# Bias products over 128 operand rows instead of two, in a recurrent-attention and mixture-of-experts block

## The reference

```
x  = x + attn(layernorm(x))
x  = x + ffn(layernorm(x))

attn(x):                                  # RWKV
    xk, xv, xr = mixes of x and x one token earlier
    k, v, r = xk Wk', xv Wv', xr Wr'
    y = wkv(-exp(time_decay), time_first, k, v)   # a scan over the 512 tokens
    return (sigmoid(r) * y) Wo'

ffn(x):
    xc = silu(pointwise(depthwise_conv3(x) + dw_bias) + pw_b)
    x1 = x + xc
    logits = x1 router_w' + router_b              # 8 experts
    rw = softmax over the two largest logits, 0 elsewhere
    ye[e] = silu(x1 expert_w[e]' + expert_b[e])   # 256 -> 256, all 8 experts
    moe = (sum over e of rw[e] * ye[e]) out_w' + out_b
    h = rmsnorm(x1 + moe) * norm_w
    return h + gelu(h ff_down_w' + ff_down_b) ff_up_w' + ff_up_b
```

## Time and profile before

| | |
|---|---|
| median of 3 runs | 1038.97 us |
| span of the profiled execution | 1038.4 us |
| mean granted TensorE clock | 0.968 of full speed |
| TensorE products (PE) | 955.6 us busy, 92%, 4288 products |
| VectorE (DVE) | 863.5 us, 83% |
| ScalarE (ACT) | 722.8 us, 70% |
| GpSimd (POOL) | 207.7 us, 20% |
| DMA | 29.66 MB, 8.4% of the 16 queues' time |

### The profile page before, as it was taken

The page is one execution under the profiler, slowest core; times in us unless marked ns, Lnnn a source line. Parts: engine busy times, 40 slices in busy tenths (PEclk is TensorE's granted clock), DMA queues, the critical chain, the costliest instruction groups (busy, mean ns, idle before and its releaser), DMA issues.

```text
span 1038.4 us, 15789 instructions
## 1 busy us (share of the span) xinstructions
PE 955.6 (92%) x4288; PEld 470.2 (45%) x4288; DVE 863.5 (83%) x1577; ACT 722.8 (70%) x1233; POOL 207.7 (20%) x475
## 2 busy tenths in 40 slices
PE   4536999999999999999999999999999999979895
PEld 2222454454545545454444445444454545344432
DVE  4998889889898988989898888989898997957562
ACT  4664687786868787786868778686877779464532
POOL 3393302121131202112130222113120111101000
PEclk9766999999999999999999999999999999999997
DMA  6110100101010010101010010101001000100000
GB/s 198 42 40 1 41 1 1 62 1 62 0 61 0 23 38 0 61 0 61 0 57 4 0 61 0 61 0 61 0 8 53 19 24 1 41 1 21 1 21 20
DMA packets 28772, 29.66 MB, mean 29 GB/s; under 512 B 2090, under 2 KB 28484, under 8 KB 28484
## 3 DMA queue, kind: packets, MB, share of 16 engines
q1 hardware_dynamic: 28740, 29.27, 8.4%
HBM read 20.87 MB, written 8.39 MB: 28 GB/s over the span
## 4 chain that ended last, share of the span: by engine, by line
PE 81%; DVE 6%; POOL 5%; issue 4%; ACT 3%; DMA 0%; POOLq 0%; DVEq 0%; ACTq 0%; SPq 0%
PE pk L447 15%; PE pe L464 12%; PE pe L466 10%; PE pe L465 10%; PE pe L462 7%; PE po L507 6%; PE po L533 5%; PE pt L441 4%; PE pt L621 3%; POOL msp L408 1%; PE po L504 1%; PE po L501 1%; PE pt L486 1%; DVE comb L1292 1%; ACT sq L746 1%
## 5 line engine op out<-in xcount | busy, mean ns | idle before, releaser
L726 ACT ACTIVATE ye<-pe 128x512 f32<-128x512 f32 x256 | 152.7, 597 | 165.5 <-PE pe L466 152.3
L1292 DVE SCALAR_TENSOR_TENSOR comb<-ye,rw,comb 128x256 f32<-128x256 f32 x448 | 216.3, 483 | 44.9 <-ACT ye L726 30.8
L464 PE MATMUL pe<-weh,x1h 128*128 128x512 f16 x512 | 196.8, 384 | 0.0
L465 PE MATMUL pe<-wel,x1h 128*128 128x512 f16 x512 | 194.0, 379 | 0.0
L466 PE MATMUL pe<-weh,x1l 128*128 128x512 f16 x512 | 194.0, 379 | 0.0
L406 POOL TENSOR_TENSOR msv<-ms,rms_eps_c 128x2 f32<-128x2 f32 x32 | 11.4, 356 | 453.1 <-ACT sq L746 453.1
L462 PE MATMUL pe<-brow,ones 2*128 2x512 f16 x256 | 98.5, 385 | 0.0
L464 PEld LDWEIGHTS pe<-weh,x1h 128*128 128x128 f16 x512 | 49.5, 97 | 88.2 <-issue 58.0
L377 POOL TENSOR_TENSOR mo<-st 128x4 f32<-128x4 f32 x32 | 11.2, 348 | 339.1 <-DVE st L1098 181.8
L466 PEld LDWEIGHTS pe<-weh,x1l 128*128 128x128 f16 x512 | 50.1, 98 | 60.5
L447 PE MATMUL pk<-xk,wa 128*128 128x512 f32 x128 | 65.2, 657 | 11.3 <-issue 8.5
(11 more groups left out here) (152 smaller groups left out, 1946.7 us busy)
## 6 DMA issues: line engine op xcount, KB each, us to landing
xa<-in_x SPq DMA_DIRECT2D x16, 512.0 KB, 3.6
xres<-in_x SPq DMA_DIRECT2D x16, 512.0 KB, 4.4
out_y<-yo SPq DMA_DIRECT2D x16, 512.0 KB, 2.9
ye<-in_w_expert SPq DMA_DIRECT2D x2, 1024.0 KB, 6.7
wa<-in_w_attn SPq DMA_DIRECT2D x1, 1024.0 KB, 7.5
wpw<-in_w_pw SPq DMA_DIRECT2D x1, 256.0 KB, 7.1
wout<-in_w_out SPq DMA_DIRECT2D x1, 256.0 KB, 6.3
wdown<-in_w_down SPq DMA_DIRECT2D x2, 64.0 KB, 5.0
```

The costliest lines, as they stand in the source:

```text
L464: nc.tensor.matmul(dst, x1h[:, h, tok], weh[:, h, cols], start=False, stop=False)
L465: nc.tensor.matmul(dst, x1h[:, h, tok], wel[:, h, cols], start=False, stop=False)
L726: act.activation(ye[:, i % NY, :], pe[:, i % 2, :], ACT.Silu, scale=1.0 / WSCALE).then_inc(ye_ready.sem, 1)
L1292: v.scalar_tensor_tensor(out=comb[:, t, :], in0=src, scalar=rw[:, t, e:e + 1], in1=comb[:, t, :], op0=ALU.mult, op1=ALU.add).then_inc(comb ...
```

## The change

`brow` and `ones2` get 128 rows instead of two. Both are first set to zero over all rows by GpSimd; then rows 0 and 1 of `ones2` are set to one, and the DMAs fill rows 0 and 1 of `brow` as before. The three bias products, whose code is the same, now read 128 rows; rows 2 to 127 add zero times zero. `pool_const` counts two more steps, and SyncE waits for it before it fills `brow`.

```diff
--- before.py
+++ after.py
@@ -90,8 +90,8 @@
         bias = sb("bias", [BP, NROW // BP])
         bias_h = sb("bias_h", [BP, NROW // BP], F16)
         bias_l = sb("bias_l", [BP, NROW // BP], F16)
-        brow = sb("brow", [2, NROW], F16)
-        ones2 = sb("ones2", [2, P], F16)
+        brow = sb("brow", [P, NROW], F16)
+        ones2 = sb("ones2", [P, P], F16)
         one = sb("one", [P, 1])
         normw = sb("normw", [P, C])
         ident = sb("ident", [P, P])
@@ -187,7 +187,7 @@
         bias_in = sig("bias_in", 16 * 2)
         stage_in = sig("stage_in", 16)
         decay_exp = sig("decay_exp", 1)
-        pool_const = sig("pool_const", 12)
+        pool_const = sig("pool_const", 14)
         early_const = sig("early_const", 1)
         dve_const = sig("dve_const", 1)
         weh_ready = sig("weh_ready", H)
@@ -331,13 +331,14 @@
             def gather_biases():
 
                 sp.wait_ge(dve_const.sem, BIAS_CONST)
+                sp.wait_ge(pool_const.sem, pool_const.per)
                 for row, part in ((0, bias_h), (1, bias_l)):
                     for c0, c1 in ((0, OB), (OB, NROW)):
                         sp.dma_start(brow[row:row + 1, c0:c1].rearrange("a (p k) -> a p k", p=BP),
                                      part[:, c0 // BP:c1 // BP]).then_inc(brow_in.sem, 16)
 
                 sp.wait_ge(brow_in.sem, 16 * 4)
-                sp.dma_start(wul[HID:HID + 2, :], brow[:, UB:UB + C]).then_inc(brow_in.sem, 16)
+                sp.dma_start(wul[HID:HID + 2, :], brow[0:2, UB:UB + C]).then_inc(brow_in.sem, 16)
 
             schedule(sp, body, {-4: stage_experts, -3: gather_biases})
             sp.wait_ge(stored.sem, stored.at(B - 1))
@@ -355,13 +356,15 @@
             nc.gpsimd.memset(ln_eps_c[:], LN_EPS * C).then_inc(pool_const.sem, 1)
             nc.gpsimd.memset(quarter_c[:], C / 4.0).then_inc(pool_const.sem, 1)
             nc.gpsimd.memset(rms_eps_c[:], RMS_EPS * C).then_inc(pool_const.sem, 1)
-            nc.gpsimd.memset(ones2[:], 1.0).then_inc(pool_const.sem, 1)
+            nc.gpsimd.memset(ones2[:], 0.0).then_inc(pool_const.sem, 1)
+            nc.gpsimd.memset(brow[:], 0.0).then_inc(pool_const.sem, 1)
             nc.gpsimd.memset(wscale[:], WSCALE).then_inc(pool_const.sem, 1)
             for e in range(NE):
                 ins = nc.gpsimd.memset(rank[:, :, e:e + 1], float(NE - e))
             ins.then_inc(pool_const.sem, 1)
 
-            pool.wait_ge(pool_const.sem, pool_const.per - 1)
+            pool.wait_ge(pool_const.sem, pool_const.per - 2)
+            nc.gpsimd.memset(ones2[0:2, :], 1.0).then_inc(pool_const.sem, 1)
             nc.gpsimd.memset(ffh[HID:, :], 1.0).then_inc(pool_const.sem, 1)
             pool.wait_ge(pool_const.sem, pool_const.per)
```

## The result

The changed kernel takes 982.18 us, the median of 4 runs (982.05 to 983.38), beside 1039.61 for the kernel before on the same chip. The ratio is 0.9454, with a 95% interval of 0.9441 to 0.9468: 5.5% faster. The forecast was 981, in a range of 970 to 1000. The span of the profiled execution is 980.4 us against 1038.4, so the traces differ by 58.0 us. Every execution that has both its time and its span on record takes 1.8 us more than its span.

A forecast was written before the change was run, and what follows sets the result against it. TensorE was taken to set the pace, VectorE next. Gains of 3.2 + 12 x 3.8 + 1.1 + 4.8 + 3.8 = 58.5 us off the 1038.4 span, plus 0.6, gave 980.5, stated as 981, range 970 to 1000.

The forecast's parts named there:

- The price of the row change: TensorE's bias products: 0.21 us per expert group and output mix, 0.17 per router product, 4.88 a sequence.
- Step 1: Router in the loop pass: it ends 0.70 us earlier, and VectorE, idle 1.43 before copying the logits, follows by 0.70.
- Step 2: Start of expert group 4: ScalarE's SiLU of group 2 holds it, 0.73 us earlier, 0.9 becoming a new TensorE wait.
- Steps 3 and 4: Groups 4 to 15 and first mix: keys 3.57 us earlier; VectorE's idle 1.22 and 1.68 used up.
- Step 5: End of the pass: squares 3.83 us earlier release the next hh transposes; a pass gains 3.8 and takes 55.6.
- sequence 13: Drain pass: pointwise product waits for VectorE's convolution, so only 0.7 plus 0.42 of the second mix, 1.1 us.
- The start: First sequence: group 4 gains 0.35 us; with 2.42 and 0.42 behind it, 3.2.
- the rows are not the cause: Rival: the two operand rows do not cause the longer starts, so the time stays 1039 us; chance 3%.
- only one of the two sides goes: Rival: only the cost of coming to or of leaving the product goes, half the sum, about 1008 us; chance 1%.
- TensorE's whole gain: Rival: TensorE keeps all it saves through the kernel, 961 to 970 us; chance 6%.
- VectorE taking over fully: Rival: VectorE or ScalarE bounds the pass, gaining 2.6 to 3.3 us; 987 to 995, up to 1003; chance 16%.
- The slower case: Rival: penalty stays and the 128 x 2568 memset delays the first statistics, 1041 to 1043 us; chance 2%.

The follow-up runs named there:

- run 6: Changed kernel with the experts' bias products back to two rows, router and output mix still at 128; 1015.71 us, ratio 0.9768.
- run 10: Changed kernel with VectorE's convolution in the drain moved from behind the combines of group 14 to those of group 12; 978.92 us, ratio 0.9415.
- run 11: Changed kernel with 15 unread TensorE products of 512 columns put into the drain's wait for the convolution; 978.54 us, ratio 0.9409.
- run 1: Changed kernel with all three bias products cut back to two rows, tensors, memsets and SyncE's wait kept; 1040.96 us, ratio 1.0007 to before.
- run 2: Changed kernel with all three bias products reading rows 0 to 63; 1041.35 us, ratio 1.0007 to before.
- run 3: Changed kernel with all three bias products reading rows 0 to 64; 981.85 us, ratio 0.9443 to before.
- run 8: Changed kernel with one VectorE instruction among the combines (num + vv) cut to 16 columns, numerator incomplete; 978.54 us, ratio 0.9412.
- run 4: Kernel before, with each of the experts' two-row bias products split into two of 256 columns; 1041.78 us, ratio 1.002.
- run 5: Changed kernel with 128 rows for the experts alone, router and output mix back to two rows; 1007.14 us, ratio 0.9682.
- run 7: Changed kernel with ScalarE's tanh of the router's gap moved behind the SiLU of group 2 and one normalisation; 978.37 us, ratio 0.9408.

## Why the prediction was right

**Step by step in the pass.** The price of the row change was right: all starts are 0.21 to 0.22 apart, and a group of seven products takes 1.51 us. Step 1 (the router hands 0.70 to VectorE) was 0.70. Step 2 had the right wait at the wrong size: 0.53 instead of 0.9. I had counted on TensorE reaching the end of group 3 with its full gain, but it loses 0.40 before group 2, since the SiLU of group 0 stands behind a copy and a table load on ScalarE and begins 13.00 us after the pass's first transposes in both traces. The one wait swallows the other. Group 4 begins 0.67 earlier instead of 0.73. Steps 3 and 4 followed from it: the scan of the keys 3.35 earlier instead of 3.57, VectorE's two idle times used up, 0.26 left instead of 0. Step 5 came out at 4.0 instead of 3.8, and not by its own way. It had the squares release the next hh transposes through GpSimd and VectorE, 3.83 earlier. The squares end 3.72 earlier, but GpSimd's first instruction behind them ends with one of VectorE's `cv` (run 6). VectorE is only 3.35 earlier, and one `cv` less is waited for, 0.66. That was not foreseen, and that it covers the 0.2 missed before is luck.

**From the span to the time.** The prediction added 0.6 us to the span, the distance of the profiled span from a median of other executions. It is 1.8 in every execution that has both. With it the sum gives 981.7.

**The ends.** This is where the working failed, unseen in the sum. For sequence 13 the prediction said that "only 0.7 reaches" the pointwise product, "and 0.42 of the second mix: 1.1". The 0.7 was exact: from the hh transposes to the product it is 43.85 us after and 44.55 before. What I did not ask is what TensorE does with the 3 us that VectorE does not follow. They became idle time, 3.85 us, the clock fell to its lower level, and the pass was 1.5 longer than before. Runs 10 and 11 show it: with the wait shortened or filled the pass takes 51.0 or 52.6. In the pass of 14 the clock is low a little longer (granted 0.93 on average against 0.97 before), and that of 15 has full clock where before it had 0.95; 3.6 and 4.6 stand for 4.8 and 3.8. About 1 us of the 4.6 belongs to that one trace of before: in run 1, whose products are those of before, the pass of 15 takes 45.9. The start holds: from the first pointwise product to the first hh transposes it is 55.2 us before and in run 1, and 51.9 with the change, 3.3 less for the forecast's 3.2. That the three drain passes were 3.0 under the forecast, the twelve passes 1.7 and the last stretch 0.9 over it, is luck of the sum.

**The rivals.** That the rows are not the cause is excluded by runs 1 to 3, and that only one of the two sides goes by the starts, which are plain on both. TensorE's whole gain would have been 4.88 a pass; 4.0 were measured. VectorE taking over fully would have left a gain of 2.6 to 3.3 a pass, and run 8, where VectorE has 1.1 us less to do and the pass stays, excludes it. The slower case needed a memset of 5.7 us; it took 2.24.

## What to carry to other kernels

Where a product over few rows stands among products over 128, read the distance between starts on both sides of it; if it is longer, pad the operands with zero rows until they pass 64. It costs memory and a memset, and no columns. Where one engine's gain is handed to another only in part, ask what the first does in the rest: if it is TensorE and the rest is one long wait, its clock may fall, as it did here at waits of 2.9 to 3.9 us, and the gain turns into a loss. The busy share does not tell which engine bounds a pass: here one that was 95% busy could lose 1.1 us of work for nothing. An instruction of GpSimd that lasts longer in one trace than in another may be waiting: look at what VectorE finishes just before its end.

## What the runs showed of the hardware

- The extra time is a step in the number of rows: 0.10 us to come and 0.10 to go at 2 and at 64 rows, none at 65, 66 and 128.
- It is paid per change, not per product (run 4).
- Behind an idle time of 3.85 us TensorE's clock was at its lower level, and a step of the f32 product took 0.85 us instead of 0.43; so it was behind 3.45 (run 5) and 2.91 (run 8), and behind 1.64 (run 10) and 0.86 it was not. How long it stayed low differed: behind the same 3.85 the four steps took 3.78 in the changed kernel and 2.55 in run 7. In the drain of both kernels the steps of the feed-forward's down product also took 0.85, behind two idle times of 1.6 and 2.6 us with one microsecond of transposes between.
- Products that nobody reads kept the clock up, and the profiled execution was 3.6 us shorter than that of the changed kernel.
- GpSimd's `msv`, 0.20 us at its shortest, took up to 1.35 us and then ended 0.05 to 0.06 behind the end of an instruction of VectorE, in all 14 traces (run 6).
